# Gathering the rows of both edge ends in column parts of 76 and 120, and making layer 3's list between the two parts of the relational tiles

## What is computed

```python
h = relu(layernorm(x))
# layer 2, for each edge e
xs, y = h[src], h[dst]
c = w_comp[etype]                                   # 16 coefficients
msg = sum_b c[b] * (xs @ weight[b])                 # 16 bases of 32 x 32
a = tanh(relu(sum((xs@A1.T + A1_b) * (y@A2.T + A2_b + rel_emb[etype])) / sqrt(32)))
nei = segment_sum(a * msg, dst)
curr = h[src[last edge of dst]] @ self_loop_weight
x = x + relu(where(in_degree > 0, nei + curr, 0))
# layer 3: ten steps of h = 0.9 * norm * (A @ (norm * h)) + 0.1 * h0
```

## Time and profile before

| | |
|---|---|
| runs | 2845.17, 2845.92, 2847.24 us |
| profiled execution | 2844.62 us, span 2842.8 us |
| VectorE busy | 1730.3 us (61%) |
| GpSimd busy | 1957.6 us (69%), 1883 instructions |
| TensorE busy | 409.5 us (14%) |
| ScalarE busy | 328.4 us (12%) |
| chain that ended last | POOL 42%, DVE 26%, issue 19%, PE 8% |
| source gathers of x_rows (L1514) | 196, 195.3 us, mean 997 ns |
| destination gathers of x_rows (L1514) | 196, 210.3 us, mean 1073 ns, idle before them 114.3 us |
| sends (L1520, i_outS) | 196, 235.9 us, mean 1203 ns, idle before them 90.2 us |
| granted TensorE clock | 1.00 |

### The profile page before, as it was taken

How to read it: one execution, slowest core, us unless ns; L and a number is a source line. 1 busy time by engine, 2 the same in 40 slices (tenths; PEclk the granted TensorE clock), 3 DMA queues, 4 the chain that set the end, 5 groups by cost and what they waited for, 6 DMA issues and landing times.

```text
span 2842.8 us, 14520 instructions
## 1 busy us (share of the span) xinstructions
PE 409.5 (14%) x2009; PEld 196.8 (7%) x2009; DVE 1730.3 (61%) x2983; ACT 328.4 (12%) x1029; POOL 1957.6 (69%) x1883
## 2 busy tenths in 40 slices
PE   0000000000000000000000004983991000160000
PEld 0000000000000000000000001331330000160000
DVE  8998898995268797113994616888889613500000
ACT  0000022110001110000110002442440100000000
POOL 6666677777746770677777777457668776757776
DMA  1001011311101310001221000000000200100000
GB/s 20 15 10 26 15 59 49 85 31 30 13 8 59 139 45 33 10 11 44 49 67 31 6 3 3 2 3 8 7 7 29 91 8 5 43 6 11 8 8 5
DMA packets 70954, 78.34 MB, mean 28 GB/s; under 512 B 38106, under 2 KB 63928, under 8 KB 69608
## 3 DMA queue, kind: packets, MB, share of 16 engines
q0 software_dynamic: 59456, 23.50, 6.3%
q1 hardware_dynamic: 5576, 28.67, 2.6%
q10 hardware_dynamic: 5856, 25.60, 2.4%
HBM read 36.82 MB, written 48.69 MB: 30 GB/s over the span
## 4 chain that ended last, share of the span: by engine, by line
POOL 42%; DVE 26%; issue 19%; PE 8%; DMA 2%; POOLq 1%; ACT 1%; DVEq 1%; ACTq 0%; SPq 0%
POOL mf L1514 12%; POOL out L1520 10%; POOL pay L1514 7%; DVE mf L491 6%; POOL xs L1514 6%; POOL xd L1514 4%; DVE pay L491 3%; POOL x_rows L1520 3%; PE psum L1934 2%; PE psum L1968 2%; PE psum L1935 2%; DVE outs L491 1%; DVE z L1336 1%; POOL z L1514 1%; POOLq L1514 1%
## 5 line engine op out<-in xcount | busy, mean ns | idle before, releaser
L1520 POOL DMA_INDIRECT out<-outs,i_outS x196 | 235.9, 1203 | 90.2 <-issue 49.2
L1514 POOL DMA_INDIRECT xd<-x_rows,i_dstX x196 | 210.3, 1073 | 114.3 <-DVE z L1336 67.3
L1514 POOL DMA_INDIRECT xs<-in_x,i_src x196 | 219.3, 1119 | 90.5 <-issue 55.6
L1514 POOL DMA_INDIRECT xd<-in_x,i_dst x196 | 205.7, 1050 | 107.9 <-DVE mf L491 44.4
L1520 POOL DMA_INDIRECT out<-outs,i_srcX x196 | 205.6, 1049 | 99.3 <-issue 56.3
L1514 POOL DMA_INDIRECT mf<-x_rows,i_srcX x196 | 195.3, 997 | 64.6 <-issue 64.6
L1514 POOL DMA_INDIRECT pay<-payload_by_dst,i_rank x196 | 195.2, 996 | 63.7 <-issue 63.7
L491 DVE TENSOR_TENSOR mf<-mf 128x128 f32<-128x128 f32 (+5 forms) x577 | 175.0, 341 | 10.4
L491 DVE TENSOR_TENSOR pay<-psum,pay 128x512 f32<-128x512 f32 x196 | 132.3, 688 | 48.4 <-ACT pay L1818 48.4
L1514 POOL DMA_INDIRECT mf<-l_own_rows,lists x124 | 123.6, 997 | 52.5 <-issue 37.5
L1514 POOL DMA_INDIRECT mf<-l_first_rows,lists x124 | 125.1, 1009 | 37.8 <-issue 37.8
(11 more groups left out here) (465 smaller groups left out, 2403.7 us busy)
## 6 DMA issues: line engine op xcount, KB each, us to landing
z<-in_x ACTq DMA_DIRECT2D x16, 624.0 KB, 5.2
out<-z ACTq DMA_DIRECT2D x16, 624.0 KB, 3.1
l_first_rows<-mf SPq DMA_DIRECT2D x2, 3234.0 KB, 9.8
l_own_rows<-pay SPq DMA_DIRECT2D x1, 3626.0 KB, 11.0
l_own_rows<-pay SPq DMA_DIRECT2D x1, 3330.0 KB, 10.0
payload_by_dst<-z SPq DMA_DIRECT2D x1, 3234.0 KB, 9.8
x_rows<-z SPq DMA_DIRECT2D x1, 3234.0 KB, 10.8
xd<-in_x,i_dst POOLq DMA_INDIRECT x196, 2.4
```

The costliest lines, as they stand in the source:

```text
L1514: G.indirect_dma_start(out=dest(k), out_offset=None, in_=table, in_offset=bass.IndirectOffsetOnAxis(ap=idx[:, k:k + 1], axis=0), bounds_ch ...
L1520: G.indirect_dma_start(out=table, out_offset=bass.IndirectOffsetOnAxis(ap=idx[:, k:k + 1], axis=0), in_=source(k), in_offset=None, bounds_ ...
```

## The change

Source and destination rows come by parts: 76 source columns, 76 destination columns, 120 source columns, 120 destination columns. In the second part, the first 90 gathers go at once, the next 72 each wait for one more finished tile, and the last 78 wait for links of the list (five for two gathers, at most to its end). The turns are split 18 and 31 instead of 24 and 25. VectorE takes the pointers of each part for itself (`pointers`), and makes layer 3's list between turn 17 and `l2_inputs(1)`; TensorE's loop is cut there and `compact_list` put between. The sends 0 to 133 are paced by the second part's tiles, 11 sends to 10 tiles, and none of them is free before that; the last 62 go at once.

```diff
--- before.py
+++ after.py
@@ -45,12 +45,12 @@
 DROWS = DCH * DCHUNKS
 TAIL_P, TAIL_C = 32, 5
 assert P * DROWS + TAIL_P * TAIL_C == N
-L2_PARTS = ((0, 100), (100, EC))
+L2_PARTS = ((0, 76), (76, EC))
 XS_PARTS = ((0, 140), (140, 180), (180, EC))
 OWN_PARTS = ((0, 180), (180, EC))
-L2_TURNS = ((0, 24), (24, EC // 4))
-FREE_ROWS, ROWS_PACE = 24, 1.25
-FREE_SENDS, SENDS_BESIDE = 40, 150
+L2_TURNS = ((0, 18), (18, EC // 4))
+ROWS_FREE, ROWS_BESIDE = 90, 72
+SENDS_BESIDE = 134
 FILLS_LISTING, FILLS_PLACING = 20, 16
 AHEAD = 13
 SORT_PACE = (("sorting", "merging", 3), ("merging", "resorting", 2), ("resorting", "sorted", 3))
@@ -1278,12 +1278,14 @@
             root(col("dis"), col("dcnt"))
 
             link(V.tensor_copy(col("dst_out"), icols["outD"][:]))
-            for part, (lo, hi) in enumerate(L2_PARTS):
+            link(V.memset(XY[:, EC:EC + 2, :], 0.0))
+
+            def pointers(part):
+
+                lo, hi = L2_PARTS[part]
                 dve.wait_ge(s[f"x2src_in{part}"], 16 * (hi - lo))
-            link(V.tensor_copy(col("kn"), XY[:, 0:EC, D]))
-            link(V.tensor_copy(icols["l3"][:], col("kn")))
-            link(V.memset(XY[:, EC:EC + 2, :], 0.0))
-            compact_edges(col("kn"), col("own"), wt)
+                link(V.tensor_copy(col("kn")[:, lo:hi], XY[:, lo:hi, D]))
+
             dve.wait_ge(s["dense_out"], 16 * (DCHUNKS + 1))
             dve.wait_ge(s["s2_stored"], 16)
 
@@ -1316,6 +1318,7 @@
                 halves_of(xy16[:, :, 2 * D:3 * D], xy16[:, :, 3 * D:4 * D], z)
                 V.tensor_copy(small[:, 2:3], small[:, 3:4]).then_inc(s["l2_xin"], 1)
 
+            pointers(0)
             l2_inputs(0)
 
             types = iota_r.unsqueeze(1).to_broadcast([P, 4, NREL])
@@ -1363,6 +1366,11 @@
                     l2_turn(last - 1, 0, False)
 
             l2_turns(*L2_TURNS[0])
+            pointers(1)
+            marks["ends"] = link.n
+            link(V.tensor_copy(icols["l3"][:], col("kn")))
+            compact_edges(col("kn"), col("own"), wt)
+            marks["ended"] = link.n
             l2_inputs(1)
             l2_turns(*L2_TURNS[1])
             dve.wait_ge(s["l2_scored"], EC // 4 + 1)
@@ -1601,24 +1609,28 @@
                 pool.wait_ge(s["s2_stored"], 32)
 
             pool.wait_ge(s["s_final"], 1)
+            tiles_before = 4 * L2_TURNS[1][0]
+            issued = 0
             for part, (lo, hi) in enumerate(L2_PARTS):
-                gather(lambda k: XY[:, k, 0:X2W], x2_dram, icols["srcX"], P * EC - 1, s[f"x2src_in{part}"], hi - lo, lo)
-            tiles_before = 4 * L2_TURNS[1][0]
-
-            for part, (lo, hi) in enumerate(L2_PARTS):
-                for k in range(lo, hi):
-                    if part == 1 and k >= lo + FREE_ROWS:
-                        pool.wait_ge(s["l2_done"], 2 + int((k - lo - FREE_ROWS) * ROWS_PACE))
-                    gather(lambda k: XDW[:, k, :], x2_dram, icols["dstX"], P * EC - 1, s[f"x2dst_in{part}"], 1, k)
-            assert (L2_PARTS[1][1] - L2_PARTS[1][0] - FREE_ROWS) * ROWS_PACE < tiles_before
+                for dest, idx, landed in ((lambda k: XY[:, k, 0:X2W], "srcX", "x2src_in"), (lambda k: XDW[:, k, :], "dstX", "x2dst_in")):
+                    for k in range(lo, hi):
+                        if part == 1:
+                            if ROWS_FREE <= issued < ROWS_FREE + ROWS_BESIDE:
+                                pool.wait_ge(s["l2_done"], 2 + issued - ROWS_FREE)
+                            elif issued >= ROWS_FREE + ROWS_BESIDE:
+                                links_done = 5 * (issued - ROWS_FREE - ROWS_BESIDE + 1) // 2
+                                pool.wait_ge(s["dve"], min(marks["ends"] + links_done, marks["ended"]))
+                            issued += 1
+                        gather(dest, x2_dram, icols[idx], P * EC - 1, s[f"{landed}{part}"], 1, k)
+            assert ROWS_BESIDE <= tiles_before
 
             pool.wait_ge(s["dense_out"], 16 * (DCHUNKS + 1))
 
             for part, (lo, hi) in enumerate(L2_PARTS):
                 pool.wait_ge(s["outs_ready"], part + 1)
                 for k in range(lo, hi):
-                    if FREE_SENDS <= k < SENDS_BESIDE:
-                        pool.wait_ge(s["l2_done"], 2 + tiles_before + (k - FREE_SENDS) * 10 // 11)
+                    if k < SENDS_BESIDE:
+                        pool.wait_ge(s["l2_done"], 2 + tiles_before + k * 10 // 11)
                     scatter(out, lambda q: OUT[:, q, :], icols["outS"], N - 1, s["outs_scattered"], 1, k)
             pool.wait_ge(s["l3_zero"], 1)
             pool.wait_ge(s["l3_own_stored"], 16)
@@ -1915,7 +1927,6 @@
                 with pe.Fori(0, L1_STEPS) as i:
                     carry(s["carry1_in"], s["carry1_out"], i + 1)
             first_keys(2)
-            compact_list(8, wcarry[:], wt)
 
 
             def turn_tile(turn, b, ahead=1):
@@ -1939,7 +1950,12 @@
                     T.matmul(PSm[b % 2], xyt[b], rxy_low, start=False, stop=True).then_inc(s["l2_mm"], 1)
 
             turn_tile(0, 0, 2)
-            with pe.Fori(0, EC // 8) as i:
+            split = L2_TURNS[1][0] // 2
+            with pe.Fori(0, split) as i:
+                for half in range(2):
+                    l2_turn(2 * i + half, half)
+            compact_list(8, wcarry[:], wt)
+            with pe.Fori(split, EC // 8) as i:
                 for half in range(2):
                     l2_turn(2 * i + half, half)
             l2_turn(EC // 4 - 1, 0)
```

## The result

The changed kernel takes 2827.07 us, median of 6 runs (2825.81 to 2828.64), against 2845.6 for the kernel before beside it (6 runs, 2844.7 to 2847.54): ratio 0.9933, 95% interval 0.9921 to 0.9946. So it is faster, by 18.5 us (0.7%); the forecast was 2819, by 27. The profiled execution took 2826.41 (span 2824.7) against 2844.62 (span 2842.8).

What follows compares the result with a forecast made beforehand. VectorE's two waits on GpSimd's gathers, then its tiles, then GpSimd's sends bound the stage; tiles end 40.8 us earlier, sends add 13.7, sum -27.1, forecast 2819 us (2812 to 2827 by itself), range 2804 to 2837.

Steps and rivals of the forecast that it cites:

- Two waits of 122 us: VectorE's waits for the last source row (48.29) and first destination rows (73.92) become one of 81 us.
- The chain of VectorE: From layer 3's keys: 76-column inputs end at 1573.5, 18 turns at 1706.6, the list at 1740.7.
- the part that steps along with the list never acts: Last 78 gathers: their list waits hold 0 to 1 us; without them the forecast is the same within 1 us.
- The gathers' sum: GpSimd's 392 gathers at 1.301 us each plus 15.9 held up: last gather at 1849.7, released 1852.2.
- Stretching by VectorE: Gathers beside VectorE's inputs are held up 5.2 + 2.6 + 8.1, in all 15.9 us.
- The tail: Sends behind the last tile: 57.6 left instead of 47, 13.7 us more, ending at T' + 101.0.
- the last paced send, column 133: In the sends: it asks for 192 finished tiles, one turn before the last tile, at T' - 7.1.
- The wide pass: VectorE's pass that needs all sends is covered by 120 following gathers of GpSimd, 156 us.
- Less held up: Rival: only the three casts hold gathers, 5.0 us in place of 15.9, giving 2808; chance 0.11.
- The tile waits hold: Rival: first tiles start later than 1609, so gathers wait for tiles, 2825 to 2845; chance 0.10.
- Held up throughout, slower: Rival: all 240 second-part gathers go at the rate beside the inputs, 79 us more, 2882; chance 0.07.
- GpSimd idles for 33 us at the third send: Behind the gathers, the third send waits some 33 us for a second-part tile; claimed to cost nothing by itself.

Runs made afterwards that it cites:

- first experiment: The changed kernel without any waits ahead of the second part's gathers, neither by tiles nor by list steps: 2824.15 us, ratio 0.9934.
- 100 and 96 columns: The changed kernel with the old part sizes, 100 and 96: with paced sends 2806.98 us, ratio 0.9875; without any pace 2752.57 us, ratio 0.9680.
- the kernel without the low half: The changed kernel with the low f16 half of the source rows set to zero by a memset, removing a two-SBUF-input instruction: 2817.24 us, one run.
- either half of the change alone: Against the kernel before: only the list moved, 2879.03 us, ratio 1.0128; only the gathers' new order, list ahead of the first inputs, 2886.51 us, ratio 1.0146.

## Why the prediction was right, and where it missed

**The mechanism held.** Two waits of 122 us become one that GpSimd's sum of 392 gathers sets; behind the last tile the longer second part leaves more sends, and these set the end. The chain of VectorE came as worked out: inputs of 76 columns to 1574.00 (1573.5), 18 turns to 1707.28 (1706.6), the list to 1741.45 (1740.7). The waits ahead of the gathers cost nothing and do nothing (first experiment), so the part that steps along with the list never acts, as said. The sizes came less well: 18.5 us were gained of 27, and 2827.07 lies at the edge of the 2812 to 2827 that the forecast had for itself, inside the range of 2804 to 2837.

**The gathers' sum was 6.0 us short**: the last starts at 1855.66, not 1849.7. Stretching by VectorE was right, 16.5 us against 15.9. The terms that were missing: the two idle spells, 2.96 and 2.90 us over the usual 0.30, which I had not seen although the trace before has them in runs of more than 113; the pitch between (1.3034 for 1.3006, 1.1 us over the run), which is scatter from profile to profile, as other kernels with the same gathers have 1.3007 to 1.3028. The start was 1.4 us earlier, the other way. From the landing of the rows to the last tile it took 249.3 us instead of 250.4. So the last tile was at 2107.48 for 2102.6, **4.9 us** late.

**The tail was 3.2 us short.** 59 sends are left behind the last tile, not 57.6. I had the last paced send, column 133, start 7.1 us ahead of it; but column 131 started there (2100.39), and 133 stood behind it and 132 and started 4.2 us ahead. With the part of the send that was under way 59.7 were left, 2.1 more than the sum had, and at 1.29 us that is 2.7 us of the miss. The first long send took 7.31 us for 7.06; the other 0.3 us stay open. The own rows' gathers begin 104.2 us behind the last tile, not 101.0.

**The wide pass** waited 9.7 us for the last send to land and had cover, as said: from the own rows' gathers to the end it takes 611.7 us where this wait is absent (sends unpaced) and 612.1 where it is 42.0 (100 and 96 columns, paced). The changed kernel's profile has 613.0 there, 0.9 more than the 612.1 before; the first experiment's kernel, whose wait is the same 9.7, has 612.1, so this is scatter. -27.1 + 4.9 + 3.2 + 0.9 = -18.1 us of span, the measured difference.

**The rivals.** *Less held up* (2808) falls: 16.5 us of stretch were measured, and the kernel without the low half shows that a two-input instruction does hold. *The tile waits hold* falls, with the first experiment: no wait acts. *Held up throughout, slower* (2882) falls: beside tiles and list the pitch is 1.3034. That a slower result was near is shown in another place, though: either half of the change alone is 35 to 42 us slower than before, and by the mechanism that the sum had, what VectorE waits for.

**What I didn't ask.** The sum took sizes and pace as given. The pace of the sends is worth 37 us, and by the kernel with 100 and 96 columns 54 us; sizes and pace together 72 (by the two ratios, 0.9933 and 0.9680) to 75 us (by the medians), four times what the change itself gains. The clue was in the prediction: GpSimd idles for 33 us at the third send and is paced at the later ones, in a stage whose end is the end of the sends. I wrote that this costs nothing by itself. That was wrong: each us of idling ahead of the last tile that a send could have filled comes back behind it, one to one, until the own rows' store is the bound. In the paced kernel with 100 and 96 columns GpSimd idles 56 us in the sends ahead of the last tile, and without the pace the own rows' gathers come 55.4 us closer behind it (84.8 for 140.2). Of the 72 us the new sizes alone, with the pace that goes with them, are 17.

## What to carry over

A wait on one engine for a queue of DMAs is read as a sum over the queue's issues; find the place of the first item that is needed, and count the issues ahead of it. Two edits that lose alone can gain together, so a change of order is costed with what it lets move. When an engine whose work forms the tail of a stage idles on purpose ahead of it, take the pace away first and look whether the other engine slows at all; here it did not.

## What the runs showed of the hardware

- Ahead of the 114th indirect DMA in an unbroken run that adds to one semaphore GpSimd stands still for about 3 us (2.9 to 4.5 with the issue time), in all thirteen profiles; spread over two semaphores the spell is gone (2752.57 to 2749.51 us).
- A gather of 128 rows beside a wide VectorE instruction with two SBUF inputs takes what that instruction has left and 0.9 us: 4.64 us, and 1.00 us where it is gone. Beside one that reads SBUF and PSUM it takes 1.00 us.
- Gathers and sends at full rate did not slow the tiles: the last tile ended at 2107.4 and at 2107.48 with the sends unpaced and paced, and 729.5 and 730.6 us behind the first gather in the kernels with 100 and 96 columns.
- On two chips VectorE issued short instructions 1.40 us apart in stretches outside the tiles, and the whole kernel took 6 to 7% longer, the kernel before too.
